# Sixteen order edits in a decoder layer: gates, context's low part, broadcasts, moves, y's second half, token turns

## The reference, cut to what matters

```python
h = x * rsqrt(mean(x*x) + 1e-6) * norm_w           # attention: 8 heads of 64
q, k, v = heads(h @ Wq.T), heads(h @ Wk.T), heads(h @ Wv.T)
q, k = rope(q), rope(k)
beta, ig, og = sigmoid(h @ Wbeta.T + bbeta), sigmoid(h @ Wig.T + big), sigmoid(h @ Wog.T + bog)
M_t = beta_t * M_(t-1) + ig_t * scale * outer(k_t, v_t)     # scan over tokens
y_t = (q_t @ M_t) * og_t
x = layernorm(x + y @ Wout.T + bout)
r_t = 0.9 * r_(t-1) + ctx_t * ctx_t                         # scan over tokens
x = layernorm(x + x * r_t)
xn = layernorm(x) * gamma + beta                            # 8 experts, 512 tokens each
x = layernorm(x + gelu(xn @ w1[e] + b1[e]) @ w2[e] + b2[e])
```

## Time and profile before

| | us |
|---|---|
| median of 3 runs (lowest, highest) | 1237.32 (1235.83, 1238.31) |
| the profiled execution's own time | 1238.27 |
| its span, first to last instruction | 1236.5 |
| PE busy | 1214.1 (98% of the span) |
| DVE / POOL / ACT busy | 789.0 (64%) / 739.7 (60%) / 455.4 (37%) |
| PE clock, in tenths of full speed, all 40 slices | 9 |
| DMA, mean rate | 145 GB/s |

### The profile page before, as it was taken

One profiled execution on the slowest core, in us unless ns is written; L12 is line 12 of the kernel. 1 busy time (PEld: TensorE's weight loads), 2 busy tenths in 40 slices (PEclk: granted clock), 3 DMA queues, 4 the chain that ended last, 5 costly groups with the idle time before them and its releaser, 6 DMA issues.

```text
span 1236.5 us, 18974 instructions
## 1 busy us (share of the span) xinstructions
PE 1214.1 (98%) x6682; PEld 1009.4 (82%) x6682; DVE 789.0 (64%) x1201; ACT 455.4 (37%) x597; POOL 739.7 (60%) x519
## 2 busy tenths in 40 slices
PE   8988999999999999999999999999999999999998
PEld 7877888888888888778888888888888888888886
DVE  5898898989898999844534544634634535445424
ACT  5223333333333332544434443534434444344420
POOL 4876666666666665568357275294385384472651
PEclk9999999999999999999999999999999999999999
DMA  8777877877777776526325235155073073162310
GB/s 283 158 152 166 166 162 156 163 165 163 164 161 165 163 161 134 172 103 246 102 83 213 87 122 193 69 183 189 13 254 128 0 280 102 55 232 96 121 50 34
DMA packets 178106, 179.51 MB, mean 145 GB/s; under 512 B 44732, under 2 KB 121484, under 8 KB 178060
## 3 DMA queue, kind: packets, MB, share of 16 engines
q1 hardware_dynamic: 177548, 178.64, 52.9%
q10 hardware_dynamic: 512, 0.26, 0.1%
HBM read 137.55 MB, written 17.18 MB: 125 GB/s over the span
## 4 chain that ended last, share of the span: by engine, by line
PE 57%; DVE 1%; POOL 0%; ACT 0%; issue 0%; POOLq 0%; DVEq 0%; ACTq 0%
PE score_ps L87 7%; PE score_ps L89 7%; PE score_ps L88 7%; PE v_ps L87 5%; PE v_ps L89 5%; PE qk_ps L89 5%; PE qk_ps L88 5%; PE v_ps L88 5%; PE qk_ps L87 5%; PE y_ps L87 2%; PE y_ps L88 2%; PE y_ps L89 2%; DVE stats_b L1299 0%; ACT xn L802 0%; DVE yT_lo L1138 0%
## 5 line engine op out<-in xcount | busy, mean ns | idle before, releaser
L1013 POOL TENSOR_TENSOR w_lo<-w_raw,w_hi 128x2048 fp32r<-128x2048 f32 x31 | 143.2, 4620 | 97.9 <-ACT w_hi L767 97.9
L1342 DVE CAST hid_hi<-score_ps 128x512 fp32r<-128x512 f32 x62 | 42.8, 690 | 192.9 <-ACT score_ps L807 192.9
L1095 DVE TENSOR_TENSOR_SCAN decays<-f_all,diag 128x384 f32<-128x384 f32 x128 | 157.6, 1270 | 0.6
L1005 POOL TENSOR_TENSOR w_lo<-w_raw,w_hi 128x2048 fp32r<-128x2048 f32 x32 | 147.6, 4614 | 12.3 <-ACT w_hi L777 12.3
L87 PE MATMUL qk_ps<-xT_parts,wqkv_hi 128*128 128x256 f32 x512 | 147.3, 288 | 2.5 <-ACT c_both L695 1.5
L88 PE MATMUL qk_ps<-xT_parts,wqkv_hi 128*128 128x256 f32 x512 | 144.7, 283 | 0.0
L89 PE MATMUL qk_ps<-xT_parts,wqkv_lo 128*128 128x256 f32 x512 | 144.7, 283 | 0.0
L1342 DVE CAST hid_hi<-v_ps 128x512 fp32r<-128x512 f32 x62 | 42.7, 689 | 142.2 <-ACT v_ps L807 142.2
L807 ACT ACTIVATE v_ps<-v_ps,b_cols 128x512 f32<-128x512 f32 x64 | 42.4, 662 | 191.3 <-PE v_ps L89 191.2
L87 PEld LDWEIGHTS qk_ps<-xT_parts,wqkv_hi 128*128 128x128 f32 x512 | 97.8, 191 | 11.2 <-issue 5.5
L807 ACT ACTIVATE score_ps<-score_ps,b_cols 128x512 f32<-128x512 f32 x64 | 42.2, 659 | 171.2 <-PE score_ps L89 170.2
(11 more groups left out here) (233 smaller groups left out, 3172.7 us busy)
## 6 DMA issues: line engine op xcount, KB each, us to landing
w_raw<-in_w SPq DMA_DIRECT2D x64, 1024.0 KB, 7.5
f_all<-f_dram SPq DMA_DIRECT2D x16, 1024.0 KB, 5.0
qkT<-rot SPq DMA_DIRECT2D x256, 64.0 KB, 2.0
xT_raw<-in_xT SPq DMA_DIRECT2D x16, 512.0 KB, 12.3
x_both<-in_x SPq DMA_DIRECT2D x16, 512.0 KB, 11.1
f_all<-f_dram SPq DMA_DIRECT2D x16, 512.0 KB, 6.1
c_both<-in_ctx_in SPq DMA_DIRECT2D x16, 512.0 KB, 12.9
x_both<-x_dram SPq DMA_DIRECT2D x8, 1024.0 KB, 4.9
```

The lines of the kernel that those rows point to most:

```text
L1005: pool.tensor_tensor(w2_lo[s % 2][:], w2_raw[s % 2][:], w2_hi[s % 2][:].bitcast(F32), ALU.subtract)\
L1013: pool.tensor_tensor(w1_lo[s % 2][:], w1_raw[s % 2][:], w1_hi[s % 2][:].bitcast(F32), ALU.subtract)\
L1095: dve.tensor_tensor_scan(decays[:, n, :], f_all[:, n, :], diag[:], 0.0, ALU.mult, ALU.add).then_inc(decay_done, 1)
L1342: dve.tensor_copy(high, up_ps[c % 2][:]).then_inc(hid_hi_done, 1)
```

## The change

Nothing is computed otherwise; operations change places in the engines' own orders, and two waits move with them.

```diff
 SP, move:        -if r != 1 or b.n == 0:            # wait for rot_done
                  +if r != 1 or b.n <= 1:
 SP, body(1), after store_rms(2), load_ctx(1), move 0:
-spread_rms(2); load_xT(3); load_x(3); move 2; move 1; move 3
-gamma, beta, b1; store_o(2); spread_f(2); load_g(2); spread_o(2)
+move 1; spread_rms(2); load_xT(3); move 2; move 3; spread_f(2)
+load_x(3); store_o(2); load_g(2); spread_o(2); gamma, beta, b1
 ACT, body:
-if (b - 2).within(B) and b.n <= B and c == (2 if b.n == B else 0):
+if (b - 2).within(B) and b.n <= B - 1 and c == 0:
     scale_x2(b - 2)
-if b.n == B - 1 and c == 2:
+if b.n == B - 1 and c == 3:          # now behind y_high(14, 1)
     expert_normalize(Step(0), 0)
 if b.n == B and c in (1, 3):
     gelu(Step(0), c // 2)
+if b.n == B and c == 3:              # now behind y_high(15, 1) and that gelu
+    scale_x2(b - 2)
...
+if (b + 1).within(B):
+    gate(b + 1)
 if b.n == 1:
     grow_memory(b - 1)
-if (b + 1).within(B):
-    gate(b + 1)
 POOL, rotate:
-if b.n >= 1 and r in (0, 2):
-    pool.wait_ge(s_mm, (b - 1).after(KC, r + 2))
+if b.n >= 1 and r == 0:
+    pool.wait_ge(s_mm, (b - 1).after(KC, 2))
+elif b.n >= 1 and r == (1 if b.n == 1 and b.i is None else 2):
+    pool.wait_ge(s_mm, (b - 1).after(KC, KC))
 POOL, body(1), behind x_low(2):
-residual(1); rotate 2; context_low(0); rotate 3
+context_low(0); rotate 2; rotate 3; residual(1)
 DVE, second (body 1):
-scans(b, 4, 5, 6, 7); sum_gates(b + 1)
+scans(b, 4); sum_gates(b + 1); scans(b, 5, 6, 7)
 DVE, middle, last (body 15), behind rope_parts 2 and 3:
-scans(b, 4); y_low(b - 1, 1); gate_v(b, 1); scans(b, 5)
+y_low(b - 1, 1); gate_v(b, 1); scans(b, 4, 5)
 PE, body(15), behind project_out(14):
-cross_memory(14); turn_tokens 2, 3
+turn_tokens 2, 3; cross_memory(14)
```

More of the change, by code:

```diff
@@ L441, in move @@
                 n, g = 1 - r // 2, r % 2
-                if r != 1 or b.n == 0:
+                if r != 1 or b.n <= 1:
                     sp.wait_ge(rot_done, b.after(NB, r + 1))
@@ L487, in body @@
                     move(b, 0)
+                    move(b, 1)
                     spread_rms(b + 1)
                     load_xT(b + 2)
+                    move(b, 2)
+                    move(b, 3)
+                    spread_f(b + 1)
                     load_x(b + 2)
-                    move(b, 2)
-                    move(b, 1)
-                    move(b, 3)
+                    store_o(b + 1)
+                    load_g(b + 1)
+                    spread_o(b + 1)
                     sp.dma_start(gamma_sb[:], gamma).then_inc(e_const_in, 16)
@@ L496, in body @@
                     sp.dma_start(b1_cols[:], b1).then_inc(e_const_in, 16)
-                    following(b + 1)
                     return
@@ L956, in body @@
                     x_low(b + 1)
-                    residual(b)
+                    context_low(b - 1)
                 if b.n == B - 1:
@@ L961, in body @@
                     rotate(b, 2)
-                    if b.n == 1:
-                        context_low(b - 1)
                     rotate(b, 3)
+                if b.n == 1:
+                    residual(b)
                 if b.n == 0:
@@ L1229, in second @@
                 rope_parts(b, 3)
-                scans(b, 4, 5, 6, 7)
+                scans(b, 4)
                 sum_gates(b + 1)
+                scans(b, 5, 6, 7)
                 add_residual(b - 1, 0)
@@ L1257, in middle @@
                 rope_parts(b, 3)
-                scans(b, 4 if last else 6)
+                if not last:
+                    scans(b, 6)
                 y_low(b - 1, 1)
@@ L1261, in middle @@
                     gate_v(b, 1)
-                    scans(b, 5)
+                    scans(b, 4, 5)
                     add_residual(b - 1, 0)
@@ L1611, in body @@
                     project_out(b - 1)
-                if b.n in (1, B - 1):
-                    cross_memory(b - 1)
                 if b.n == B - 1:
@@ L1616, in body @@
                     turn_tokens(Step(0), 3)
+                if b.n in (1, B - 1):
+                    cross_memory(b - 1)
             def turn_tokens(e, k):
```

## The result

The changed kernel takes 1240.11 us (median of 20 runs, 1237.35 to 1242.3) and the kernel before 1236.76 (20 runs on the same chip, 1234.45 to 1238.31): a ratio of 1.0027 [1.002, 1.0034]. It is slower, where 1235.8 was forecast and 1238.4 was the upper end. Its profiled execution took 1241.66 us, 1.55 above that median, with a span of 1239.9.

The account below looks back on a forecast made before the run. PE was taken as the bound, busy 1214.1 of 1236.5 us, with waits giving a 10.6 us ceiling. +1.1 and -2.6 sum to -1.5: 1238.27 to 1236.8 profiled, median 1235.8, range 1232.4 to 1238.4.

Parts of the forecast that it names:

- The 4.6 us at the gate: Before body 2, PE waits for grow_memory(0), queued behind gate(2): resumes at 72.1 instead of 67.48, 4.6 us lost (3.4 to 6).
- The 0.85, 2.1, 1.50, 1.85 and the last body's 1.28: PE waits in us, the first three in bodies 1 to 3, the others in bodies 15 and 16, forecast to go.
- The last bodies: Bodies 15 and 16: two gains of 1.3 us each, together -2.6 us (-1.9 to -3.9).
- y's second half: Body 15: y_high ahead of expert_normalize removes PE's 1.85; head 6's held scan limits the gain to 1.3 of 2.8 us.
- scale_x2: Last body: scale_x2(14) queued behind y_high(15, 1) removes PE's 1.28 wait wholly, -1.3 us.
- the token turns: Body 15: turns placed before cross_memory(14) take their own wait from ACT, earning nothing while scan 6 is held.
- Broadcasts and moves: Body 2: spread_f(2) lands at 79.1, x(3) later at 80.7, POOL late; cross_memory(1) at 99.5, 2.6 us behind before.
- the sign that I had set: Forecast is wrong in its size if cross_memory(1) starts before 98 or after 101.
- the forecast's +1.1: Sum for bodies 1 to 3: 2.6 us lost at cross_memory(1) less 1.5 before 105.48, +1.1 us (-1.3 to +4.6).
- A: Body 2: POOL not late, x(3) lands by 77, cross_memory(1) at 97.1; 1233.4 us in total; chance 0.30.
- B: o_tables(2) to last rope part: POOL's lateness grows, x(3) landing after 82.4; 1239.3 us; chance 0.13.
- C: Both stages: DVE follows PE so closely that waits only move; gain 0 to 0.5, 1237.0 us; chance 0.12.

Follow-up runs that it names:

- swap_alone: Kernel before with one edit: on ACT, gate(2) ahead of grow_memory(0); ratio 1.0013 [1.0001, 1.0024].
- end_scan6: Kernel before with all edits of bodies 15 and 16, plus head 6's scan of batch 15 moved to just ahead of head 7's; 0.9957, 1231.38 us.
- end_scale: Kernel before with only scale_x2(14) moved behind y_high(15, 1) and the gelu; ratio 0.9995 [0.9983, 1.0006].
- x_before_f: Changed kernel with one exchange on SP: load_x(3) issued ahead of spread_f(2); ratio 0.9991 [0.9979, 1.0002].
- grow_first: Changed kernel with ACT's grow_memory(0) ahead of gate(2) again, all else kept; ratio 1.0017.
- after: The changed kernel itself, with all edits, against the kernel before; 1240.11 us, ratio 1.0027 [1.002, 1.0034].
- start_only: Changed kernel with the edits of bodies 15 and 16 undone, so only those of body 1 remain; ratio 1.0039.
- sp_alone: Kernel before with only SP's new order of body 1 and the moved waits of move and rotate; ratio 1.0044.
- warm: Changed kernel with 28 thrown-away identity matmuls on PE between cross_memory(0) and body 2; ratio 1.0038 [1.0024, 1.0052].
- x_warm: x_before_f with 28 thrown-away identity matmuls on PE behind cross_memory(0); ratio 1.0014 [1.0004, 1.0025].
- end_only: Kernel before with all edits to bodies 15 and 16 and none to body 1; ratio 0.9965.
- best_a: Changed kernel with the exchanges of x_before_f, grow_first and end_scan6 together; ratio 0.9982 against the kernel before.

## Why the prediction was wrong

**What held.** The list of waits was the right place to look, and the middle carried both differences unchanged. `gate(2)` came at 70.87 (forecast 70.1) and PE's body 2 at 72.65 (72.1); `sum_gates(2)` waited 2.75 (2 to 3); `clear_f(2)` had no wait; x(3) landed at 81.1 (80.7), `rms_scale(3)` ran at 82.94 (82.2), `o_tables(2)` at 91.81 with no wait of its own (90.2), the second rotation ended at 99.1 (98.2). The 4.6 us at the gate are lost and then for the most part absorbed: `swap_alone` costs 1.6 [0.1, 3.0]. The 0.85, 2.1, 1.50, 1.85 and the last body's 1.28 are gone, and the wait at `scores(15, 0)` was 1.28 (1.3). The last bodies, -2.6 with -1.9 to -3.9, measured -3.1 in the trace and -4.3 [-6.1, -2.5] in time. The term of *y's second half* with its held scan is shown by `end_scan6`, that of *scale_x2* by the trace of `end_scale`; the token turns were not tried by themselves.

**The step that failed** is the last one of *Broadcasts and moves*: "the second rotation ends at 98.2 [...] The last rope part needs it: 98.2 + 1.2 = 99.4. `cross_memory(1)` starts at 99.5, 2.6 behind before." It started at 102.35. I had POOL as the engine that ends last there and let DVE's scans run beside it at 0.8 each. DVE ends last: its fourth scan ended at 99.9, after the rotation, and the four rope operations took 2.4 more. (As a plain sum of its terms, 90.2 + 5.4 and four scans of 0.8, it would have been 98.8 and not 98.2.) By the sign that I had set, a start of `cross_memory(1)` after 101, the forecast is wrong in its size. What the late x(3) does is to push POOL's chain (`x_low(3)`, the layernorm scale, `context_low(1)`, `o_tables(2)`) onto DVE's own critical stretch. Before, `x_low(3)` and `context_low(1)` ran at 75.57 and 79.90, beside statistics and ropes of DVE that took no longer for it, and beside the 2.46 us in which DVE waited for f. The 3.94 us in which POOL waited for its tables lay beside the first two scans, and these took 1.81; beside `x_low(3)` they took 3.92. The token gates took 3.57 in place of 1.98 beside `context_low(1)`, the four scans 5.54 in place of 4.47: 4.8 us. That this, and not PE's lateness, is the price is shown by `x_before_f`: the same wait of 6 us before body 2, the same f queue but for one exchange, 7.8 us for the same three groups, and no wait at `cross_memory(1)`. The converse is `grow_first`: PE on time at body 2, x(3) late, and `cross_memory(1)` at 101.43 all the same. How the late POOL reaches DVE differs: in `after` and `start_only` by these three groups, in `grow_first` and `sp_alone` by the 3.3 us at `y_low(1)` and by the four scans.

I quoted the Trainium skill ("SBUF — State Buffer", shared ports) for body 15 and left it out here. The rows agree with it here as well. `x_low(3)` ran from 83.89 to 86.27, and the first two scans began at 84.01, just behind it; if they were blocked to its end and then took their 1.81, they would end at 88.1, an estimate, and they ended at 87.93. The token gates are another kind of operation (`TENSOR_SCALAR`), for which I show only the times: `context_low(1)` ended at 91.86, the pair of gates at 93.14, and POOL's first operation of `o_tables`, begun at 91.81, at 93.12. When the loser is blocked fully, each POOL operation of 2.4 us that falls into DVE's critical stretch can cost up to its whole length, which the forecast should have charged for `x_low` and `context_low`.

**The term that was missing** is the clock. The forecast has PE work at one speed; the granted clock halved behind both long waits. From `cross_memory(1)` to body 3 the changed kernel needed 9.72 us in its profiled execution; before it was 8.57, of which 1.50 were a wait, so 7.07 of work: 2.65 us more. The slow k share of body 2 (6.00 for 3.85) made DVE wait 2.54 for its scores at 79.74. Over all executions the mean clock fell from 0.998 to 0.9952, which is 2 x 0.0028 x 1240 = 6.9 us more at half speed and up to 3.5 us more of work, as much as the net loss of 3.3. The executions of the kernel before alone give the same price: over its 98 runs in the three groups, time falls by 1.2 us for each 0.001 that the mean clock is higher (1.5, 1.1 and 0.8 in the single groups; correlation -0.73 over all), which is 3.4 us for 0.0028. That is a correlation and no proof, since a longer wait costs time itself and takes the clock down too; `warm` and `x_warm`, made to part the two, did not settle it in whole time. With 2.85 at `cross_memory(1)` and 2.65 behind it, the forecast's +1.1 becomes 6.6; the trace has 6.5 with the 0.28 ahead of the stage. The 2.65 belongs to that one execution: `start_only` was spared it. The Trainium skill ("TensorE: Matmul & The Clock Gate", the part on the gate) says that the clock has the levels 1.2 and 2.4 GHz and is set by how busy PE has been of late; the rows of 0.51 and 1.00 agree. It was the rule that spoke against this change, and I had left it unweighed although I forecast a wait of 4 to 6 us.

**The profile of before was one draw of several.** The start stage is the same code in the kernel before, `end_only`, `end_scale` and `end_scan6`, and takes 44.21, 41.67, 41.50 and 42.26. The 2.1 at `v`, which I counted as cover for a late PE, is 0.3 to 0.5 in the other three. In three of four executions there were thus 1.6 to 1.8 us less to absorb with.

**The rivals.** A did not come: POOL was late. B's price (1239.3) and its place, `o_tables(2)` to the last rope part, were near the truth, and its cause was not: x(3) landed before its 82.4. Its chance of 0.13 was low because I asked only how late x(3) might be, and not which operations of DVE a late POOL would run beside. C's thought, that DVE is full and follows, is nearer to what the rows show than its price, 1237.0.

## What to carry to other kernels

A transfer moved back in a queue is to be followed through every engine that works in program order behind it, and what that engine's work then lies beside can matter as much as when it ends. A wait of PE should be priced with the clock behind it, and a row of the trace that one wants to use as slack should be seen in more than one execution. Where a wait is the longest row of a profile, take it away by itself before believing that it is the loss.

## What the runs showed of the hardware

- The granted clock went to half behind PE waits of 2.3 (`best_a`, at 105.89), 2.8, 3.2, 4.4, 6.0, 6.1 and 7.2 us, and stayed there 3.4, 6.8 or 10.2 us; behind the wait of 2.40 at 101.37 in `start_only` it did not, nor behind any of 0.3 to 2.1 in bodies 1 to 3 of the kernel before. In `x_warm` it fell at 517.0, behind waits of 1.3 and 1.7 us at 506 and 515; in `x_before_f` it stayed full behind a wait of 1.7 us at the same place. Between 10 and 22 us it was at half for 3.4 us in `warm`, `swap_alone`, `end_scan6` and `best_a`, and at full speed in the kernel before, with waits of up to 2.1 us ahead of it in all five.
- In 98 executions of the kernel before, the time was 1.2 us lower for each 0.001 by which the mean granted clock was higher.
- Two operations of DVE on 128 x 8 elements took 1.21 us in `swap_alone`, beside POOL operations of 0.7, and 3.57 beside POOL's `context_low` and `o_tables`; four scans 3.50 us alone and 6.26 beside POOL's chain.
- The same 512 KB load of x(3) landed in 3.5 us when issued ahead of `spread_f(2)`, in 6.8 behind it in the changed kernel, and in 7.6 in `sp_alone`; the issue itself was 5.1 us later in the changed kernel than in `x_before_f`.
- 28 thrown-away products in body 1 went with 1.8 to 2.0 us more in a stage that begins 470 us later; the cause is open.
